# Attention scores by two halves of the TensorE array in a fused transformer block

## The reference

```python
qkv = x @ w_qkv.T + b_qkv          # 32 query heads, 8 key and value heads, 32 features each
q, k = apply_rope(q, 0), apply_rope(k, 0)
k = jnp.repeat(k, GROUP, axis=1)   # 4 query heads share a key head
scores = jnp.einsum('bhqd,bhkd->bhqk', q, k) / math.sqrt(HEAD_DIM)
scores = jnp.where(causal, scores, -1e20)
attn = jax.nn.softmax(scores, axis=-1)
```

## Time and profile before

| | us |
|---|---|
| median of 3 runs | 1148.61 (1147.75 to 1149.65) |
| the profiled execution | 1150.56 |
| its span, first to last instruction | 1148.3 |
| busy: PE / weight loads | 1118.9 / 975.7 |
| busy: DVE / ACT / POOL | 687.0 / 423.6 / 164.6 |

### The profile page before, as it was taken

One profiled execution on the slowest core, in us unless ns is written; L12 is line 12 of the kernel. 1 busy time (PEld: TensorE's weight loads), 2 busy tenths in 40 slices (PEclk: granted clock), 3 DMA queues, 4 the chain that ended last, 5 costly groups with the idle time before them and its releaser, 6 DMA issues.

```text
span 1148.3 us, 16846 instructions
## 1 busy us (share of the span) xinstructions
PE 1118.9 (97%) x6048; PEld 975.7 (85%) x6048; DVE 687.0 (60%) x1233; ACT 423.6 (37%) x1204; POOL 164.6 (14%) x130
## 2 busy tenths in 40 slices
PE   7999999999999999999979999999999999999998
PEld 6888888888888888888878998888888888888887
DVE  5312138888888888888884235233146766666664
ACT  5312125556565566555555224111122322222221
POOL 0000112333333333333241001000000000000000
PEclk9999999999999999999999999999999999999999
DMA  8020032222222332232335116383562323332122
GB/s 290 11 71 19 10 107 80 65 64 64 64 64 64 73 72 65 66 90 55 92 114 129 57 37 193 102 236 101 140 183 60 106 111 110 110 110 96 74 70 92
DMA packets 92899, 106.69 MB, mean 93 GB/s; under 512 B 8498, under 2 KB 74930, under 8 KB 92850
## 3 DMA queue, kind: packets, MB, share of 16 engines
q1 hardware_dynamic: 90146, 97.38, 28.1%
q0 software_dynamic: 2560, 8.39, 4.4%
q10 hardware_dynamic: 144, 0.26, 0.1%
HBM read 72.45 MB, written 25.17 MB: 85 GB/s over the span
## 4 chain that ended last, share of the span: by engine, by line
PE 68%; DVE 18%; ACT 8%; issue 3%; DMA 2%; POOL 0%; DVEq 0%; SPq 0%
PE psum L1583 15%; PE psum L280 13%; PE psum L1891 12%; PE psum L1314 8%; PE psum L933 6%; ACT prob L628 5%; PE psum L1969 4%; PE psum L1871 3%; DVE roped L760 2%; DVE rot_t L760 2%; PE psum L966 2%; DVE pt_l L765 2%; DVE ssum L780 2%; DVE prob L859 2%; DVE smax L857 2%
## 5 line engine op out<-in xcount | busy, mean ns | idle before, releaser
L933 PE MATMUL psum<-p_h,c_high_low 128*128 128x512 f32 (+1 forms) x768 | 195.6, 361 | 0.5 <-POOL end_l L712 0.5
L933 PEld LDWEIGHTS psum<-p_h,c_high_low 128*128 128x128 f32 x768 | 132.3, 189 | 14.3 <-issue 0.7
L280 PE MATMUL psum<-c_high_low,w_h 128*128 128x512 f32 x384 | 120.0, 398 | 5.8 <-ACT c_high_low L215 5.8
L1583 PE MATMUL psum<-ring,rows 128*128 128x512 f32 x528 | 123.7, 392 | 1.3 <-DVE t_plain L1288 1.3
L1583 PEld LDWEIGHTS psum<-ring,rows 128*128 128x128 f32 x528 | 98.8, 188 | 24.2 <-DVE t_plain L1288 2.6
L1314 PE MATMUL psum<-chunk,rows 128*128 128x384 f32 (+1 forms) x576 | 108.6, 343 | 4.2 <-DVE rows L1182 2.5
L1314 PEld LDWEIGHTS psum<-chunk,rows 128*128 128x128 f32 x576 | 101.8, 190 | 5.4 <-issue 3.2
L933 PE MATMUL psum<-p_l,c_high_low 128*128 128x512 f32 (+1 forms) x384 | 103.0, 363 | 0.0
L280 PEld LDWEIGHTS psum<-c_high_low,w_h 128*128 128x128 f32 x384 | 73.8, 192 | 22.6 <-ACT c_high_low L215 5.8
L708 POOL TENSOR_TENSOR c_high_low<-ring_plain,c_high_low 128x512 fp32r<-128x512 f32 x32 | 41.3, 1291 | 329.8 <-ACT c_high_low L589 190.1
L628 ACT ACTIVATE prob<-prob 128x64 f32<-128x64 f32 x240 | 58.1, 244 | 54.1 <-DVE prob L859 54.1
(11 more groups left out here) (172 smaller groups left out, 2174.9 us busy)
## 6 DMA issues: line engine op xcount, KB each, us to landing
ring_plain<-in_x_t SPq DMA_DIRECT2D x32, 256.0 KB, 3.0
ring_plain<-attn_scratch SPq DMA_DIRECT2D x32, 256.0 KB, 4.0
raw<-x_t_scratch SPq DMA_DIRECT2D x16, 512.0 KB, 4.2
rest<-in_b_base SPq DMA_DIRECT2D x16, 512.0 KB, 4.4
out<-rest SPq DMA_DIRECT2D x15, 512.0 KB, 2.9
ring_plain<-in_wqkv_t SPq DMA_DIRECT2D x10, 512.0 KB, 6.1
a_raw<-in_lora_a SPq DMA_DIRECT2D x32, 128.0 KB, 2.1
ring_plain<-ring_plain POOLq DMA_DIRECT2D x16, 256.0 KB, 3.5
```

Of the source, the lines that this page charges most:

```text
L280: mm = pe.matmul(to, stationary, moving, start=k == 0 and m == 0, stop=k == KT - 1 and last, skip_group_check=True)
L933: mm = pe.matmul(to, sx[:, kk, :], moving(w, n, kk), start=first, stop=False, skip_group_check=True)
L1583: mm = pe.matmul(self.psum[:, self.BANK_OF[i], :], w[:, cols], s, start=m == 0 and p == 0, stop=m == KT - 1 and p == 2, skip_group_check=True)
```

## The change

The key copies are masked by pairs of heads instead of single heads, and each score product is replaced by two of half the rows. Partitions 0 to 63 of a quad's tile hold its heads 0 and 1, partitions 64 to 127 its heads 2 and 3. The new `pair_mask[:, c]` is `hmask[:, c] + hmask[:, c + 2]`: it keeps head c in the lower half of the rows and head c + 2 in the upper half. It is made once by DVE ahead of its steps, after a wait for the constants. There are two masked copies of the keys instead of four, in ACT (L666) and DVE (L837), and the counts of `k_high` follow.

A product now takes 64 rows: stationary 64 x 128 (queries), moving 64 x 128 (two masked keys of 64 tokens). The halves j = 0 (rows 0 to 63) and j = 1 (rows 64 to 127) alternate and write to different banks, since j now chooses the bank. That makes 24 products of 128 columns for each b, 48 for each unit, and as many weight loads. The transposes of the probabilities read the heads from their new places and have the same number and shape.

```diff
-    k_h, k_l = (sb(n, [P, QUADS, BPU, 4, SEQ], F32R) for n in ("k_h", "k_l"))
+    k_h, k_l = (sb(n, [P, QUADS, BPU, 2, SEQ], F32R) for n in ("k_h", "k_l"))
+    pair_mask = sb("pair_place", [P, 4 * QUADS * P])[:, 0:2]
...
-                for c in range(4):
-                    act.activation(k_h[:, :, :, c, :].rearrange("p q b t -> p (q b) t"), k_tiles(), ACT.Copy, scale=hmask[:, c:c + 1]).then_inc(k_high, 1)
+                for c in range(2):
+                    act.activation(k_h[:, :, :, c, :].rearrange("p q b t -> p (q b) t"), k_tiles(), ACT.Copy, scale=pair_mask[:, c:c + 1]).then_inc(k_high, 1)
...
-                for c in range(4):
-                    dve.wait_ge(k_high, 4 * v + c + 1)
-                    last = dve.scalar_tensor_tensor(k_l[:, :, :, c, :].rearrange("p q b t -> p (q b) t"), k_tiles(), hmask[:, c:c + 1],
+                for c in range(2):
+                    dve.wait_ge(k_high, 2 * v + c + 1)
+                    last = dve.scalar_tensor_tensor(k_l[:, :, :, c, :].rearrange("p q b t -> p (q b) t"), k_tiles(), pair_mask[:, c:c + 1],
...
+        dve.wait_ge(const_in, 16 * len(consts))
+        dve.tensor_tensor(pair_mask, hmask[:, 0:2], hmask[:, 2:4], ALU.add)
...
-                    o = scores_ps[b][:, g, q * 4 * SEQ:(q + 1) * 4 * SEQ]
-                    cols = slice(q * GRP + 2 * g, q * GRP + 2 * g + 2)
+                    cols, at = slice(q * GRP + 2 * g, q * GRP + 2 * g + 2), (g * QUADS + q) * P
                     for n, (qq, kk) in enumerate(((q_h, k_h), (q_h, k_l), (q_l, k_h))):
-                        mm = pe.matmul(o, qq[:, b, cols, :].rearrange("p g t -> p (g t)"), kk[:, q, b, :, :].rearrange("p c t -> p (c t)"),
-                                       start=n == 0, stop=n == 2)
+                        for j, rows in enumerate((high_rows, low_rows)):
+                            mm = pe.matmul(scores_ps[b][:, j, at:at + P], qq[rows, b, cols, :].rearrange("p g t -> p (g t)"),
+                                           kk[rows, q, b, :, :].rearrange("p c t -> p (c t)"), start=n == 0, stop=n == 2)
...
-                        c = q * 4 + j * 2
-                        mm = pe.transpose(t_ps[:, q, at:at + P], prob[:, b, g, c:c + 2, :].rearrange("p c k -> p (c k)"), ident[:, :])
+                        c = (g * QUADS + q) * 2
+                        mm = pe.transpose(t_ps[:, q, at:at + P], prob[:, b, j, c:c + 2, :].rearrange("p c k -> p (c k)"), ident[:, :])
```

## The result

| | us |
|---|---|
| changed kernel, median of 6 runs | 1153.51 (1152.15 to 1154.0) |
| before, 6 runs beside them | 1148.27 (1147.45 to 1149.65) |
| ratio, 95% interval | 1.004 (1.0029 to 1.0052) |
| span of the profiled execution | 1151.6 (before 1148.3) |

The changed kernel is slower by 5.2 us, or 0.4%. I had forecast -1.2 us.

What follows compares the result with a forecast made beforehand. PE's queue was taken to bound the kernel, busy 1118.9 of 1148.3 us. 29 blocks at -0.04 us gave -1.2 us, other terms 0: 1149.4 us profiled, 1147.4 in the median; range 1145 to 1187.

Steps and rivals of the forecast that it cites:

- Halves side by side: Score blocks on PE: a pair costs one load, 0.110 us; block 1.38 us, 0.04 us less than before; chance 0.50.
- a lag of 0.06 us: Score blocks: the second half trails by two steps of PE's queue, 0.06 us, added once to a block's 1.32 us.
- Entering and leaving: Each score block's switch of PE from whole-array products to halves and back, taken to cost 0.
- upper bound: Switches around score blocks: at most 0.27 us each for drain and uncovered load, 2 x 29 switches, 15.8 us.
- rival 2: Around score blocks, a switch drains PE: +15.8 us on -1.2, so 1163.2 us; chance 0.10, smaller drains included.
- 29 blocks count in full: Attention units: 28 blocks in units two to fifteen, one in the first, none in the sixteenth; 29 x -0.04 = -1.2 us.
- Rival 1: Score blocks: both halves' loads share one path, 2.64 us a block, +35.4 us, so 1184.0 us; chance 0.30.
- Rival 3: Score blocks: columns alone count, 0.64 us less for the first block, 13.7 us in all, so 1134.9; chance 0.07.
- Masked keys at 0: Key copies on ACT and DVE: two fewer each per unit; the 0.85 us go to waits, so cost 0.
- The sign: Whole kernel: chances of 0.20 faster, 0.37 no change (less than 0.2%, 2.3 us) and 0.43 slower.

Runs made afterwards that it cites:

- experiment 5: Kernel before with each 256-column score product made as two of 128 columns on whole rows, each with its own load: 1184.24 us, ratio 1.0308.
- experiments 1 and 2: Kernel before with one overwritten 128-column product ahead of each score block: of 64 rows in the first, 1160.13 us; of 128 rows in the second, 1149.68 us.
- experiment 6: Changed kernel with all 12 products of one half ahead of the other half's, instead of alternating: 1182.17 us, ratio 1.0295 to the kernel before.
- experiment 4: Changed kernel with POOL normalising only half of the probabilities of b = 1: 1152.96 us, ratio 1.0039 to the kernel before.

## Why the prediction was wrong

- **Halves side by side (50%).** Right. I took 0.110 us a pair from one stream of loads on whole rows and measured 0.112. The whole-row stream itself was confirmed by experiment 5. I added a lag of 0.06 us between the halves, from the first instructions of the transposes; in the changed kernel's second pair the two products start within 0.006 us of each other and the two loads within 0.004. The Trainium skill's 4 ns for products of different row groups (page "TensorE: Matmul & The Clock Gate", "Part 3: Packing small matmuls — row/col tiling") agrees with that.
- **Entering and leaving: the step that failed.** "So I take 0". The nearest row, weights of 64 columns among weights of 128, says nothing of a change of rows. A way in and out costs 0.34 us by the block's rows and 0.34 to 0.36 by experiments 1 and 2, for 0.54 in my upper bound (0.27 each way). I had the mechanism as rival 2, with a price some 60% above the one measured and at a chance of 10%, because I let a row of another kind outweigh a stated rule. The Trainium skill ("TensorEngine Tiling (Array Packing)", section "Key Properties") says that a change of tiling mode drains TensorE. For rows the trace agrees that there is a pause (0.24 us from the start of the last product to the first load of the halves, for 0.01 before the change), though that load does not wait for the end of the product's record, which is 0.31 us long; for columns no pause is seen in the earlier trace rows.
- **29 blocks count in full.** Nearly right in number, wrong in what follows a block. The first unit lost 0.03 us, and not a block's 0.26: its wait for `low` took in 0.4 of the 0.52 us, so 28 blocks count. I read PE's own list of waits, in which L1014 waits 0.2 us for lows. The weight loads' idle time (7.3 us) showed a wait of some 0.3 us a unit, which took in half of the loss; and the time that POOL and DVE then lay over each other added 0.11 us. Without both, the loss would have been 28 x 0.26 = 7.3 us; it was 5.2.
- **Rival 1 (shared load path, 30%).** Refuted by the x2 rows. Rival 3 (columns alone) too: a pair takes 0.112 us, the time of a load, and not 0.065.
- **Masked keys at 0.** Right in the cost, wrong in the waits that hide them: ACT waits 3.56 us before L629 and DVE 1.27 us before L856, for 3.50 and 1.22, and no time came back. The 0.85 us went to the waits of both engines for the last query tile, which stand earlier in their order than the two that I named: ACT's ahead of q_h (1.10 us for 0.30) and DVE's ahead of q_l (0.79 us for none).
- **The sign.** I forecast -1.2 us, which I called no change (37%), and it was +5.2 us. The 43% for slower went mostly to rival 1, a reason that did not come true. The measured time lies inside 1145 to 1187 by luck: above 1151 the range was drawn for that rival.

## What to carry to other kernels

Splitting the array by rows runs two products in the time of one load, but each way into halves and out again costs about 0.35 us of PE here: count the switches first, and put all half-row work of a stage behind each other. Where products have 128 columns and weights of their own, the load (0.11 us) is the price, so halves of 128 columns gain almost nothing on whole-row products of 256 (0.112 us a pair for 0.118 us a product). To find what absorbs a change on PE, read the idle time of the weight loads as well as that of the products.

## What the hardware showed beside this

- Two loads of 64 rows and 128 columns in different halves start together and take a pair's 0.112 us; alone, one takes 0.111 (experiment 6).
- With all of one half's products ahead of the other's, the second half ran about three products ahead of its turn and no more, in the one order tried (experiment 6).
- POOL's 1.91 us product over DVE's 0.82 us one lengthens the latter by 0.13 us for an overlap of 0.28 us; without the overlap it is back at 0.82 (experiment 4).
- A switch between weights of 64 and of 128 columns on whole rows shows no pause; one from 128 to 64 rows holds back the first load to 0.24 us after the start of the last product, for 0.01 without it.
